# A DRAM-to-DRAM cast copy of x, issued in two pieces at the start or in eight pieces during the first weight stage

## The reference

```
x = x + attn(layernorm(x)); x = x + ffn(layernorm(x))
attn: i = h Wi^T, f = h Wf^T, g = h Wg^T
      gate = sigmoid(f); o = scan(o*gate + silu(i)*(1-gate)) along the sequence
      out = g * rsqrt(mean(g^2)+eps) * g_norm * silu(o);  return out Wo^T
ffn:  top-2 of 8 experts by router logits, softmax weights,
      sum of w_e * (silu(h w1_e) * (h w2_e)) w3_e
```

## Time and profile before

| | us |
|---|---|
| median of 2 runs (4259.37 to 4262.74) | 4261.05 |
| profiled execution | 4264.51 |
| its span, slowest core (core 1) | 4262.5 |
| span of the fastest core (core 6) | 4233.0 |
| TensorE matmul busy | 3751.5 (88%) |
| VectorE busy | 1317.4 (31%) |
| software DMA queue, share of 16 engines | 36.1% |

### The profile page before, as it was taken

The page is one execution under the profiler, slowest core; times in us unless marked ns, Lnnn a source line. Parts: engine busy times, 40 slices in busy tenths (PEclk is TensorE's granted clock), DMA queues, the critical chain, the costliest instruction groups (busy, mean ns, idle before and its releaser), DMA issues.

```text
span 4262.5 us, 43591 instructions; the slowest of 8 cores (4233.0 to 4262.5 us)
## 1 busy us (share of the span) xinstructions
PE 3751.5 (88%) x18832; PEld 1771.7 (42%) x18832; DVE 1317.4 (31%) x1154; ACT 366.4 (9%) x347; POOL 325.3 (8%) x364
## 2 busy tenths in 40 slices
PE   0279899998982499999999999999999999999992
PEld 0145444443441244444444444444444444444442
DVE  0512255453224522322322322322232232232232
ACT  0222112120002000000000000000000000000000
POOL 0000000000001000100000110010010010010011
PEclk9989899999995699999999999999999999999995
DMA  9852312111239234344343343344343344343238
GB/s 143 202 90 35 54 31 38 33 20 20 35 80 168 24 35 40 35 43 42 30 42 36 38 42 38 32 40 40 35 45 35 35 40 40 35 45 35 28 35 158
DMA packets 416556, 221.00 MB, mean 52 GB/s; under 512 B 399456, under 2 KB 399456, under 8 KB 409712
## 3 DMA queue, kind: packets, MB, share of 16 engines
q0 software_dynamic: 413616, 184.61, 36.1%
q1 hardware_dynamic: 2752, 33.61, 3.5%
HBM read 327.28 MB, written 58.72 MB: 91 GB/s over the span
## 4 chain that ended last, share of the span: by engine, by line
PE 79%; DMA 8%; DVE 8%; another core or an unknown queue 2%; ACT 2%; issue 1%; DVEq 0%; POOL 0%; ACTq 0%; SPq 0%; POOLq 0%
PE pga L838 21%; PE pva L853 21%; PE pw L932 19%; PE po L580 5%; PE pg L339 5%; DMA y<-gvw 4%; PE pi L480 3%; PE pf L480 3%; DVE fsc L512 2%; DMA fsc<-x 1%; PE pw L904 1%; DMA wsc<-wg 1%; DVE bufB L520 1%; DVE fsc L519 1%
## 5 line engine op out<-in xcount | busy, mean ns | idle before, releaser
L838 PE MATMUL pga<-bufA,wsc 128*128 128x512 bf16 x4096 | 913.0, 381 | 0.0
L853 PE MATMUL pva<-bufA,wsc 128*128 128x512 bf16 x4096 | 904.9, 379 | 0.0
L932 PE MATMUL pw<-gvw,wsc 128*128 128x512 bf16 x3840 | 830.8, 379 | 2.8 <-DMA wsc<-w 2.8
L838 PEld LDWEIGHTS pga<-bufA,wsc 128*128 128x128 bf16 x4096 | 402.2, 98 | 491.1 <-issue 14.4
L853 PEld LDWEIGHTS pva<-bufA,wsc 128*128 128x128 bf16 x4096 | 400.7, 98 | 483.4
L932 PEld LDWEIGHTS pw<-gvw,wsc 128*128 128x128 bf16 x3840 | 375.3, 98 | 457.0 <-issue 5.4
L772 POOL DMA_DIRECT2D wsc<-w x256 | 258.1, 1009 | 2463.4 <-PE pga L838 1180.6
L944 DVE TENSOR_TENSOR bufB<-pw,bufB 128x1024 bf16<-128x1024 f32 x224 | 274.3, 1225 | 496.1 <-PE pw L932 470.5
L865 DVE TENSOR_TENSOR gvw<-fsc,pga 128x1024 bf16<-128x1024 f32 x128 | 156.3, 1221 | 786.1 <-ACT fsc L861 786.1
L861 ACT ACTIVATE fsc<-pga 128x1024 f32<-128x1024 f32 x128 | 131.1, 1024 | 2455.3 <-PE pga L838 2455.3
L869 DVE TENSOR_TENSOR scr<-pva,fsc 128x1024 bf16<-128x1024 f32 x128 | 156.8, 1225 | 577.3 <-PE pva L853 577.3
(11 more groups left out here) (116 smaller groups left out, 1440.0 us busy)
## 6 DMA issues: line engine op xcount, KB each, us to landing
wsc<-w POOLq DMA_DIRECT2D x128, 512.0 KB, 6.4
y<-gvw POOLq DMA_DIRECT2D x32, 1024.0 KB, 12.8
wsc<-w POOLq DMA_DIRECT2D x128, 256.0 KB, 4.4
fsc<-x SPq DMA_DIRECT2D x16, 1024.0 KB, 6.8
wsc<-wg POOLq DMA_DIRECT2D x16, 512.0 KB, 5.1
wsc<-wo POOLq DMA_DIRECT2D x16, 512.0 KB, 5.1
gvw<-wi POOLq DMA_DIRECT2D x16, 512.0 KB, 5.0
gvw<-wf POOLq DMA_DIRECT2D x16, 512.0 KB, 6.7
```

The lines of the kernel that those rows point to most:

```text
L838: ins = e.matmul(out=pga[:, n2 * 512:(n2 + 1) * 512], lhsT=lhsT, rhs=bufA[:, k * 2048 + nn:k * 2048 + nn + 512], start=(k == 0), stop=(k = ...
L853: ins = e.matmul(out=pva[:, n2 * 512:(n2 + 1) * 512], lhsT=lhsT, rhs=bufA[:, k * 2048 + nn:k * 2048 + nn + 512], start=(k == 0), stop=(k = ...
L932: ins = e.matmul(out=pws[_sl][:, n2 * 512:(n2 + 1) * 512], lhsT=lhsT, rhs=gvw[:, k * 2048 + nn:k * 2048 + nn + 512], start=(k == 0), stop= ...
```

## The change

The two DMAs ahead of stage B0 are gone. In the loop over m, every turn with even m issues one DMA of 256 rows (part j = m/2, so eight parts), right after the issue of the load of Wg block m+1. All eight raise the one semaphore `xq0`, and the wait ahead of the loads of `bufB` asks for its full count. Part 0 falls in turn 0, where the load of block 1 waits for nothing.

```diff
-        xq0.n += 16
-        on("gpsimd", lambda e, _h=xq0.h: e.dma_start(
-            out=xbf_d[0:4 * 128, :], in_=xin[0:4 * 128, :]).then_inc(_h, 16))
-        xq1.n += 16
-        on("gpsimd", lambda e, _h=xq1.h: e.dma_start(
-            out=xbf_d[4 * 128:16 * 128, :], in_=xin[4 * 128:16 * 128, :]).then_inc(_h, 16))
...
             for m in range(TEm):
                 if m + 1 < TEm:
                     wg_slots[m + 1] = rowblock_into(wgs, wg_d, m + 1, natsl[(m + 1) % 2])
+                if m % 2 == 0:
+                    j = m // 2
+                    xq0.n += 16
+                    on("gpsimd", lambda e, _j=j, _h=xq0.h: e.dma_start(
+                        out=xbf_d[_j * 256:(_j + 1) * 256, :],
+                        in_=xin[_j * 256:(_j + 1) * 256, :]).then_inc(_h, 16))
                 wait("tensor", ve, copy_ev[m])
...
             wait("gpsimd", te, TE_B3)
-            wait("gpsimd", xq0, 16)
-            wait("gpsimd", xq1, 16)
+            wait("gpsimd", xq0, xq0.n)
```

## The result

| | before | changed |
|---|---|---|
| median, us (all runs) | 4264.86 | 4199.29 |
| ratio, 95% interval | | 0.9847 (0.9834 to 0.9861) |
| profiled execution, us | 4264.51 | 4195.63 |
| span of the slowest core (core 1) | 4262.5 | 4194.0 |
| last x tile used by VectorE, core 1 | 156.25 | 88.16 |

The ratio is 65 us of 4262. It lies within 2% of no change, and its interval is clear of 1. The forecast was 66 us less, 4195 us.

A forecast was written before the change was run, and what follows sets the result against it. The start was taken as bound by x loads waiting for DMA engines busy with the xbf copy. Removing seven parts gave 65.8 us, the other steps 0: 4261 - 66 = 4195 us, range 4178 to 4222.

The forecast's parts named there:

- Step 1: Start: seven of eight xbf copy parts leave it, 9.4 us of DMA engine time each, 65.8 us gained.
- The second way of working it: Start, from tile times: tile 2 used at 25.1 us, tile 15 at 87.4, which is 68.9 us earlier.
- Step 2: Start: Wg blocks 0 and 1 go ahead of part 0; their landing early is worth nothing.
- the bounds: Gain at the start: 78.3 us if part 0 is hidden, 53.1 if it and two Wg loads cost landing time.
- Step 3: Up to 256.6 us: all shifts rigidly by 66 us; y copy still 108.6 us, TensorE's stall still 22.00 us.
- Step 4: Wg stage: parts 1 to 7 cost nothing; part and next load take 14.5 to 20.1 of 30.2 us cover.
- Rival D: Wg stage: parts make blocks late, 4387 us; slower if a load takes over 39.6 us, 2% over 51.8; chance 0.04.
- Step 5: Wg stage: part 1, issued while the y copy runs, costs 0, at most 9.4 us.
- rival A: Before Wg block 2: part 1 stretches the y copy and TensorE's stall by 9.4 us, 4204 us; chance 0.14.
- Rival B: Wg stage: seven parts hold up instruction fetches, 5.64 us each, 39.5 us in all, 4234 us; chance 0.08.
- Rival C: Start: the xbf copy does not hold the x loads, or the time comes back elsewhere, 4261 us; chance 0.04.
- Rival E: Start and y copy: full 78.3 us and the 22.00 us stall both go, 100.3 us, 4161 us; chance 0.04.

The follow-up runs named there:

- e2: Changed kernel with all eight copy parts in turns 4 to 11 of the Wg stage, none at the start; 0.9818 of the kernel before.
- e3: Changed kernel with four copy parts at the start and four in turns 4, 6, 8 and 10; 0.9914 of the kernel before.
- e1: Changed kernel with all eight copy parts at the start, ahead of Wg blocks 0 and 1; 1.0017 of the kernel before.
- e4: Changed kernel with the whole copy as one DMA in turn 4 of the Wg stage; 4234.6 and 4235.9 us.
- e11: Changed kernel with the copy as two DMAs of 1024 rows in turns 4 and 10, none at the start; 4189.7 us.
- e5: Changed kernel with the y copy cut into 16 DMAs, one per turn of the Wi/Wf stage; 0.978 of the kernel before.
- e6: Changed kernel with four x buffers in stage 1 instead of two; 0.984 of the kernel before.

## Why the prediction was right

**Step 1, the parts taken out of the start.** It said 65.8 us, last tile at 85 to 92. It was 68.1 us on core 1 (156.25 to 88.16), 66.5, 63.0 and 63.4 us on cores 3, 5 and 7, and the slope over e2, e3, e1 is the term itself. That forecast and ratio agree to 1 us is partly luck: the interval is some 6 us wide each way, and the cores scatter by 5. The second way of working it came out near by two errors that cancel. Tile 2 was used at 32.56 us, not 25.1, outside the 25 to 30 that were to show step 1: part 0 took 27.7 us to land, behind two Wg blocks, and the tile waited. From tile 2 to tile 15 it was then 55.60 us, not 62.29. The two Wg loads no longer fell into that stretch, which fits, but was not tested by itself. Engine time, which asks for no order, was the better term.

**Step 2, Wg blocks 0 and 1 ahead of the parts.** Nobody missed them, as said. Their cost was in the bounds and is inside the two figures above.

**Step 3, the rigid shift.** The y copy was issued 67.3 us sooner and took 109.5 us (108.6 before). The stall was 23.89 us, 1.9 more than before, and the first 32 matmuls after it 8.69 us instead of 7.69. At the transposes of block 4 the lead is 289.61 - 224.49 = 65.1 us. Then the shift is not rigid: 60.6 us at the first transpose of B3 (1255.4 against 1194.8), 63.8 at the first matmul of the experts, 67.1 at the last stage (4164.0 - 4096.9) and 68.5 at the end. What moves it there is not shown; the step had no term for it.

**Step 4, the parts under the Wg stage.** Right that they cost nothing, and wrong in one size: the cover of a part is 45 us, not 30.2 (e4, e11). The step counted from the issue of the next block, but a part is issued a whole block (15.6 us) before that. For the part and the load behind it together, 14.5 to 20.1 us, some 25 us of cover remained at worst and not 10; the error was on the safe side. Rival D's points of 39.6 and 51.8 us are times of a load from its own issue, for which 30.2 us is right: in e4 block 6 was issued at 221.46 and wanted at 251.2.

**Step 5 and rival A, part 1 beside the y copy.** Part 1 landed at 154.27 + 48.9 = 203.2 us, 13 us after the y copy and 8 after block 3 (153.75 + 41.0 = 194.8), which fits ring order. e2, e4 and e11 have no part there, and on their odd cores (5 and 7 in e2) the y copies take 109.5 to 112.3 us and the stalls are 23.0 to 26.6; in the changed kernel 109.4 to 110.1 and 23.8 to 24.4. So part 1 has no cost that can be seen, and the 1.9 us lie within the spread of the kernel before over its odd cores (22.0 to 25.2).

**Rival B, instruction fetches.** No stop of more than 0.22 us with no releaser in the Wg stage, with one part or with the whole copy in flight (e4). The stop in the first transposes went with the y copy (e5), and on core 1 the one packet of the instruction queue q8 near the stop lies inside it: between 199 and 200 us in the kernel before (stop 196.1 to 201.8), between 131 and 132 in the changed kernel (128.1 to 133.5). That TensorE waited for this fetch, and why the Wg stage is spared, is not shown.

**Rival C** fell with e1 to e3. **Rival D**: one part is far from the point, the whole copy beyond it (e4). **Rival E**: the stall did not go along; it takes moving the y copy (e5), and then the time is 2.2% below the kernel before.

## What to carry to other kernels

A background copy is free only where the DMA engines have time; price it by its share of engine time (here 9.4 us per 256 rows, with the neighbour core doing the same), not by its issue cost, and move it to a stage whose share is low. Behind it in its ring every load waits its full length, so count the cover from the copy's issue to the moment when the next load is needed. And look at what the saved time runs into: here first another copy, then the neighbour core.

## What the runs showed of the hardware that was not expected

- The last stage of a pair of cores ends 114 to 122 us after its first core began it, with leads from 3 to 31 us (13 kernels). A gain that only brings the two closer together is mostly lost in it (12 us in stage 1, 3 us at the end, e6).
- In that stage a core with full DMA engines moves 154 to 166 GB/s while its neighbour is in it too, and 245 to 281 alone (changed kernel, cores 0, 1, 6 and 7).
- TensorE's stop of 1.8 to 9.2 us in the first transposes stands on every core with the 16.8 MB y copy running, and on none of 32 without it.
- Two y copies of a pair that begin 1.4 us apart (e6) take 114.7 and 114.1 us; 2.3 us apart (changed kernel), with fewer x loads beside them, 106.8 and 109.5.
- Issuing the 8192 KB at the start in eight DMAs instead of two changed their cost by less than the measurement can tell (e1).
